# Nodes in 49 blocks of 128 consecutive ones, and edge loads in rows of 64, 3 and 1, in a two-layer graph network kernel

## The chip, the cores and the metric

One core of one Trainium2 chip runs the whole program. The metric is the device time of one execution in microseconds (us); lower is better. The chip's engines that matter here are PE (TensorE, matrix products and transposes), DVE (VectorE), ACT (ScalarE), POOL (GpSimd, which here issues the gathers of table rows) and SP (SyncE, which issues the other transfers in order, in one queue).

## The reference, cut to what matters

There are 6250 nodes with 64 features each and 200,000 edges, sorted by their target `dst`; `src` is random.

```python
h = jnp.maximum(_layernorm(x, axis=-1), 0.0)
# layer 0
t = h @ W0 + b0
agg = segment_sum(edge_weight[:, None] * t[src], dst)      # 6250 x 64
deg = segment_sum(edge_weight, dst)
x = x + relu(agg / (deg[:, None] + 1e-6))
h = jnp.maximum(_layernorm(x, axis=-1), 0.0)
# layer 1
m = gelu(concat(h[src], edge_attr) @ W_msg + b_msg)        # 200000 x 64
agg = segment_sum(m, dst)
x = x + gelu(((1 + eps) * h + agg) @ W_upd + b_upd)
```

## The kernel before, in words

**Edges.** The 200,000 edges are cut into `NG` = 196 groups of 1024, each as `J` = 8 columns of 128 edges. Four groups, one per slot, make a body, and each layer runs 49 bodies. For one group, the rows of the source nodes are fetched into `rows[:, slot, j, :]` in two ways. For six or seven of the eight columns, POOL issues one indirect transfer per column from a table in DRAM (L447; 26 a body in layer 0 and 27 in layer 1). The last column (in some slots the last two) is picked on chip: DVE compares the broadcast source numbers `src_bc` with the node numbers of each partition and writes 0 or 1 into `pick` (L945, function `pick_half`), and PE multiplies these with `parts`, the table split into three bf16 parts, in `NK` = 50 products that add up (L659 `gather`, L666 `extra`). DVE adds the three parts (L973, L979). The comparisons of one pair of groups are made in two halves.

**Sums by target.** Edges are sorted, so a group's targets lie in a window of 72 nodes. ACT makes the one-hot matrix (L523, L527). In layer 0 ACT weights the rows (L553), PE multiplies them with the one-hot (L693), and DVE adds the result to `sums_sb` (L995), which holds features on partitions and nodes along them. In layer 1 PE transposes the edge features (L771), multiplies them with the lower half of `W_msg` (L784, `edge_product`), DVE adds the gathered rows (L1109), and ACT applies gelu (L598). A group whose targets need more windows runs a conditional block on PE and DVE.

**Slots.** POOL fetches into slot `s` for the next body only when `s_used[s]` says that the slot's rows were read (L553 in layer 0, L1109 in layer 1) and `s_idx[s]` that the new indices are there (L461).

**Nodes.** Node `c*625 + p*5 + k` stands on partition p of 125, in chunk c of 10, at place k of 5. So a partition has five consecutive nodes of a chunk, 1280 bytes in DRAM, and a piece of `sums_sb` that belongs to one k is read with a step of five floats (L730, `v[:, k, :]`, and L299, `nodes_of`). Work on nodes goes in five units of two chunks, 640 elements a partition:
- start: SP loads x in five transfers (L310), then src, dst and edge weights, each as 128 + 67 + 1 rows of 4 KB (L314, L315, L317). DVE and ACT do the layer norm; SP stores table 0 (L338). POOL casts src and dst to float (L422 to L426) and then computes `src_last` (L431: the sources of the last two columns minus k, as 16-bit numbers, with ACT's transposed casts `take` at L490 making `src_tab`, `dst_tab` and `w_tab`); SP writes it to DRAM (L341, L343) and loads it back as a broadcast to 125 partitions (L328, L333).
- middle, between the layers: PE multiplies the sums with W0 (L732), DVE divides, adds and normalizes (L1059 to L1063, L851, L852, L858, L863), PE transposes (L751) and multiplies with the upper half of `W_msg` (L758), ACT copies the transposed nodes (L568, L569) and seeds `sums_sb` with them, 50 operations (L578), DVE writes the rows of table 1 (L1072), SP stores them (L391), and POOL starts when all is stored (L437).
- tail: PE multiplies the sums with `W_upd` (L732 again), DVE, ACT and DVE finish (L1136, L611, L1142), SP stores `out` (L406).

Of the kernel before, what the change touches and what calls it, by code (L numbers as in the profile page):

```python
# [5 lines left out]
def two_layer_gnn(  # L6
# [87 lines left out]
    last_src = nc.dram_tensor("last_src", (2, KN, NG, P), i16, kind="Internal").ap()  # L94

    x_view = x.rearrange("(c p k) d -> p c (k d)", p=PN, k=KN)
    out_view = out.rearrange("(c p k) d -> p c (k d)", p=PN, k=KN)
    h0_view = h0_table.rearrange("(c p k) d -> p c (k d)", p=PN, k=KN)
    p1_view = p1_table.rearrange("(c p k) d -> p c (k d)", p=PN, k=KN)


    UC = 2
    UNITS = NC // UC
    UN = UC * KN
    UQ = UN // 2
    UD = UN * D
    BANK = 512
    assert UC * UNITS == NC and UQ == 5
# [3 lines left out]
    with ctx:  # L112
# [3 lines left out]
        def sem(name):  # L116
# [8 lines left out]
        bm_bc = sb("bm_bc", [PN, D])  # L125
        W1b_sb = sb("W1b_sb", [P, P])
        Wu_sb = sb("Wu_sb", [P, D])
        bu_bc = sb("bu_bc", [PN, D])
# [4 lines left out]
        node_f = sb("node_f", [PN, NC])  # L133
        parts = sb("parts", [PN, NK, SPLIT * D], bf16)
        src_bc = sb("src_bc", [PN, 2, KN, PE3 + 16], i16)
        pick_all = sb("pick_all", [P, 2 * NK * PE3], bf16)
        pick = [[pick_all[:, i * NK * PE3:i * NK * PE3 + NK * (PE3 if EXTRA[layer][i] else PE2)].rearrange(
            "p (n e) -> p n e", n=NK) for i in range(2)] for layer in range(2)]
# [5 lines left out]
        def prep(flat, n):  # L144
# [9 lines left out]
        src_tab = sb("src_tab", [P, NG * J], u16)  # L154
        dst_tab = sb("dst_tab", [P, NG * J], i16)
        w_tab = sb("w_tab", [P, NG * J])
        stat = sb("stat", [P, 2, 4])
        stat_i = sb("stat_i", [P, 2, 1], i32)
        once = 10 * G + 2 * P + 2 * KN * P
# [26 lines left out]
        hT = room[:, 0:2 * UQ * PN].rearrange("p (i e) -> p i e", i=2)  # L186
# [7 lines left out]
        psM = [ps[:, 5 + h, 0:J // 2 * D] for h in range(2)]  # L194
        psR = [ps[:, 3:5, :], ps[:, 5:7, :]]
        psU = [ps[:, 1 + 2 * i:3 + 2 * i, :] for i in range(2)]
        psN = [ps[:, 1 + i, :] for i in range(2)]
        psH = ps[:, 5:7, :]
        psP = [ps[:, 0, :], ps[:, 7, :]]
        psS = ps[:, 7, :]  # L200
        psG = [ps[:, 3 + i, 0:SPLIT * D] for i in range(2)]
        psX = ps[:, 2, 0:SPLIT * D]
# [5 lines left out]
        s_wt = sem("edge_weight_loaded")  # L208
        s_const = sem("constants_ready")
# [75 lines left out]
        def unit(t, u):  # L285

            return t[:, u * UC:(u + 1) * UC, :]

        def rows3(t):

            return t.rearrange("p c (k d) -> p (c k) d", d=D)

        def split_to(u):
            return parts[:, u * UN:(u + 1) * UN, :]

        def nodes_of(n):

            c, k = n // KN, n % KN
            return sums_sb[0:D, c * CHUNK:(c + 1) * CHUNK].rearrange("f (p k) -> f k p", k=KN)[:, k, :]  # L299

        @block.sync
        def _(sp):
# [6 lines left out]
            for u in range(UNITS):  # L309
                sp.dma_start(unit(x_sb, u), unit(x_view, u)).then_inc(s_x[u], 16)  # L310
# [41 lines left out]
            sp.dma_start(bm_bc[:, :], b_msg.rearrange("(a n) -> a n", a=1).to_broadcast([PN, D])).then_inc(s_w, 16)  # L352
# [5 lines left out]
            sp.dma_start(bu_bc[:, :], b_upd.rearrange("(a n) -> a n", a=1).to_broadcast([PN, D])).then_inc(s_w, 16)  # L358
# [94 lines left out]
        def _(act):  # L453
# [50 lines left out]
            for s in range(SLOTS):  # L504
                copy_idx(s, s)
# [665 lines left out]
```

## Time and profile before

| | |
|---|---|
| time, median of 3 runs | 3411.88 us (3411.7 to 3414.16) |
| time of the profiled execution | 3412.54 us |
| its span | 3410.7 us |
| busy: PE, DVE, ACT, POOL | 3052.1, 2505.7, 1964.2, 2479.1 us |
| mean granted TensorE clock | 0.967 |
| mean DMA rate | 68 GB/s |

The span is the time from the first to the last instruction of the profiled execution. The busy time of POOL counts the gathers' own time, but not the time between them. "Granted clock" is the share of TensorE's full speed that the chip allowed.

### The profile page before, as it was taken

Reading aid. Unit: us, or ns where it says so; the run is one execution under the profiler, and the core shown is the slowest. Engines: PE = TensorE matmul, PEld = TensorE weight load, DVE = VectorE, ACT = ScalarE, POOL = GpSimd, SP = SyncE. Lnnn points to the kernel's source line nnn. Section 1 sums busy time; section 2 is a strip of 40 time slices with the busy share of each in tenths; the row PEclk is TensorE's granted clock in tenths of the full one; section 3 lists DMA queues with packets and bytes.
Section 4 is the critical chain, followed back from the end, with each engine's and each line's share of the span. In section 5 each row is a group of like instructions: output and inputs, shape, how many; then the busy total and the mean of one; then the engine's idle time right before and its main releaser. Section 6 shows DMA issues by size and latency. Waiting matters only on the chain.

```text
span 3410.7 us, 103092 instructions
## 1 busy us (share of the span) xinstructions
PE 3052.1 (89%) x37471; PEld 2931.5 (86%) x37472; DVE 2505.7 (73%) x3633; ACT 1964.2 (58%) x6688; POOL 2479.1 (73%) x2622
## 2 busy tenths in 40 slices
PE   1999999999999999999879889989999989998998
PEld 1999999999989889989778888888888888888887
DVE  5888777778778778777757767676767677777764
ACT  4666666666665666566565555555555555555553
POOL 4777777777777777777357777777777777777774
PEclk9999999999999999999789999999999999999997
DMA  3333333333333333333123333433333333333331
GB/s 90 74 60 55 57 57 54 54 56 59 54 55 58 56 54 55 57 58 55 36 67 81 80 83 79 84 80 88 76 86 81 79 82 79 81 80 81 79 82 49
DMA packets 336155, 232.77 MB, mean 68 GB/s; under 512 B 141398, under 2 KB 268898, under 8 KB 336126
## 3 DMA queue, kind: packets, MB, share of 16 engines
q0 software_dynamic: 83104, 85.26, 18.1%
q1 hardware_dynamic: 253022, 147.13, 15.6%
q8 instruction: 17, 0.28, 0.0%
q14 instruction: 12, 0.10, 0.0%
HBM read 226.91 MB, written 5.30 MB: 68 GB/s over the span
## 4 chain that ended last, share of the span: by engine, by line
POOL 35%; issue 13%; PE 1%; ACT 1%; DVE 1%; POOLq 0%; DMA 0%; DVEq 0%
POOL rows L447 35%; PE ps L732 1%; ACT sums_sb L578 0%; POOLq L445 0%; DMA p_table<-h_sb 0%; PE ps L758 0%; POOLq L438 0%; DVE pick_all L945 0%; DVE h_sb L852 0%; DVE x_sb L1063 0%; DVE h_sb L1061 0%; DVE ln_m L851 0%; DMA rows<-p_table,idx 0%; ACT sq L468 0%; PE ps L693 0%
## 5 line engine op out<-in xcount | busy, mean ns | idle before, releaser
L945 DVE TENSOR_SCALAR pick_all<-src_bc,node_f 125x1920 bf16<-125x1920 int16 (+1 forms) x1960 | 2067.4, 1121 | 44.9 <-issue 20.4
L659 PE MATMUL ps<-parts,pick_all 125*128 125x192 bf16 x19600 | 1709.8, 248 | 92.2 <-DVE pick_all L945 81.9
L659 PEld LDWEIGHTS ps<-parts,pick_all 125*128 125x128 bf16 x19600 | 1636.1, 99 | 116.0 <-DVE pick_all L945 65.6
L447 POOL DMA_INDIRECT rows<-p_table,idx x1323 | 1249.3, 944 | 424.3 <-issue 424.3
L447 POOL DMA_INDIRECT rows<-h_table,idx x1274 | 1203.2, 944 | 400.5 <-issue 400.2
L523 ACT ACTIVATE onehot<-iota,dw 128x72 f32<-128x72 f32 x3136 | 809.5, 342 | 0.0
L666 PE MATMUL ps<-parts,pick_all 125*128 125x192 bf16 x7350 | 681.4, 252 | 11.6 <-issue 11.4
L666 PEld LDWEIGHTS ps<-parts,pick_all 125*128 125x128 bf16 x7350 | 631.4, 100 | 21.7 <-issue 16.9
L598 ACT ACTIVATE room<-room 128x512 f32<-128x512 f32 x196 | 123.6, 630 | 740.4 <-DVE room L1109 740.4
L1109 DVE TENSOR_TENSOR room<-ps,rows 128x512 f32<-128x512 f32 x196 | 135.6, 692 | 466.3 <-DMA rows<-p_table,idx 437.3
L693 PE MATMUL ps<-onehot,room 128*65 128x72 f32 (+1 forms) x6272 | 381.2, 232 | 92.1 <-ACT room L553 84.6
L693 PEld LDWEIGHTS ps<-onehot,room 128*65 128x65 f32 (+1 forms) x6272 | 333.3, 139 | 136.4 <-ACT room L553 97.8
L553 ACT ACTIVATE room<-rows,dw 128x65 f32<-128x65 f32 x1568 | 397.1, 336 | 59.2 <-DVE rows L973 59.1
L461 ACT CAST idx<-src_tab 128x8 int32 (+1 forms) x392 | 75.8, 194 | 540.4 <-DMA rows<-h_table,idx 539.8
L784 PE MATMUL ps<-W1b_sb,eT 64*128 64x64 f32 x3136 | 217.5, 277 | 89.4 <-issue 88.0
L784 PEld LDWEIGHTS ps<-W1b_sb,eT 64*128 64x128 f32 x3136 | 194.9, 187 | 114.0 <-issue 103.0
L527 ACT ACTIVATE onehot<-onehot 128x576 f32<-128x576 f32 x392 | 268.0, 684 | 12.4
L995 DVE TENSOR_TENSOR sums_sb<-sums_sb,ps 65x72 f32 (+1 forms) x392 | 87.3, 223 | 253.3 <-PE ps L693 253.3
L973 DVE TENSOR_REDUCE rows<-ps 128x64 f32<-128x192 f32 x392 | 136.7, 349 | 56.9 <-PE ps L659 56.6
L771 PE MATMUL ps<-ident,ea 128*128 128x128 f32 x784 | 129.0, 287 | 1.0 <-DVE h_sb L1072 1.0
L593 ACT COPY eT<-ps 128x512 f32<-128x512 f32 x196 | 113.5, 579 | 0.5
L771 PEld LDWEIGHTS ps<-ident,ea 128*128 128x128 f32 x784 | 82.4, 141 | 14.5 <-DVE h_sb L1072 1.3
(90 smaller groups left out, 646.4 us busy)
## 6 DMA issues: line engine op xcount, KB each, us to landing
src_bc<-last_src SPq DMA_DIRECT2D x196, 312.5 KB
ea<-in_edge_attr_dram SPq DMA_DIRECT2D x196, 256.0 KB
src_bc<-last_src SPq DMA_DIRECT2D x147, 156.2 KB
rows<-p_table,idx POOLq DMA_INDIRECT x1323
rows<-h_table,idx POOLq DMA_INDIRECT x1274
x_sb<-in_x_dram SPq DMA_DIRECT2D x5, 312.5 KB
h_table<-h_sb SPq DMA_DIRECT2D x5, 312.5 KB
p_table<-h_sb SPq DMA_DIRECT2D x5, 312.5 KB
```

Of the source, the lines that this page charges most:

```text
L447: nc.gpsimd.indirect_dma_start(out=rows[:, s, j, 0:D], out_offset=None, in_=table[:, :], in_offset=bass.IndirectOffsetOnAxis(ap=idx[:, s, ...
L523: last = nc.scalar.activation(onehot[:, s % 2, j, :], iota[:, :], ACT.Abs, scale=-1.0, bias=dw[:, s, 0, j:j + 1])
L527: nc.scalar.activation(onehot[:, s % 2, :, :], onehot[:, s % 2, :, :], ACT.Relu, scale=-1.0, bias=1.0).then_inc(s_oh[layer], 1)
L553: last = nc.scalar.activation(wrows[:, s % 2, j, :], rows[:, s, j, :], ACT.Copy, scale=dw[:, s, 1, j:j + 1])
L659: last = nc.tensor.matmul(psG[(s + shift) % 2], pick[layer][(s + shift) // 2 % 2][0:PN, n, at:at + P], parts[:, n, :], start=(n == 0), sto ...
L666: last = nc.tensor.matmul(psX, pick[layer][i][0:PN, n, PE2:PE3], parts[:, n, :], start=(n == 0), stop=(n == NK - 1))
L693: last = nc.tensor.matmul(psW[s % 2][at:at + width, :], lhs(j), onehot[:, s % 2, j, :], start=(j < sets), stop=(j >= J - sets))
L771: last = nc.tensor.transpose(psT[:, q * P:(q + 1) * P], ea[:, slot, q * P:(q + 1) * P], ident[:, :])
L784: last = nc.tensor.matmul(psM[h][:, q * D:(q + 1) * D], eT[h * D:(h + 1) * D, q * P:(q + 1) * P], W1b_sb[h * D:(h + 1) * D, h * D:(h + 1) ...
L945: last = nc.vector.tensor_scalar(pick[layer][i][0:PN, c * KN:(c + 1) * KN, :], src_bc[:, i, :, 0:w], node_f[:, c:c + 1], None, ALU.is_equal)
L973: nc.vector.tensor_reduce(rows[:, slot, JG, 0:D], psG[slot % 2].rearrange("p (q d) -> p d q", q=SPLIT), AX.X, ALU.add).then_inc(s_prow[lay ...
L1109: nc.vector.tensor_tensor(pre[:, slot % 2, :].rearrange("p (q h d) -> p q h d", h=2, d=D), ps[:, 5:7, 0:J // 2 * D].rearrange("p h (q d) - ...
```

## The change

Node `n*128 + p` now stands on partition p of 128, in block n of `NB` = 49; the last block has 106 nodes and is padded with zeros. Work on nodes goes in seven units of seven blocks, 448 elements a partition. A block is a contiguous piece of 128 in `sums_sb`, and a row of 256 bytes a partition in DRAM. A pick takes 49 products and seven comparisons of 7 x 384 (or 256) elements, three in the first half and four in the second; the broadcast goes to 128 partitions with seven copies (of src - 128k) in place of five. The remaining 67 rows of an edge load are cut into 64, 3 and 1; the order of the loads is x of units 0 and 1, src, the rest of x, dst, weights. `src_last` is made by 14 ACT operations in place of ten on POOL. POOL's memset of `sums_sb` comes after the src casts. The edge tables are laid out as [column, group], so that the casts write without a step. Seeding takes two ACT operations a unit. `psM` is one bank with four products of 128 columns, not two with eight of 64, and the edge product of the next group is issued right after the first window's products, ahead of the conditional block.

```diff
+    NB = -(-N // P)
+    FULL = N // P
+    TAIL = N - FULL * P
+    KB = 7
+    UNITS = NB // KB
...
+    ROWS2 = (HALF[1] - 1) // 16 * 16
...
-        src_tab = sb("src_tab", [P, NG * J], u16)
+        src_tab = sb("src_tab", [P, J, NG], u16)
...
-        psM = [ps[:, 5 + h, 0:J // 2 * D] for h in range(2)]
+        psM = ps[:, 2, :]
...
+            def blocks(table, lo, hi):
+
+                return table[lo * P:hi * P, :].rearrange("(n p) d -> p n d", p=P)
...
             def load_edges(to, a, loaded):
                 sp.dma_start(to[:, 0, :], a[0:P * G].rearrange("(r e) -> r e", e=G)).then_inc(loaded, 16)
-                sp.dma_start(to[0:HALF[1] - 1, 1, :],
-                             a[P * G:LAST * G].rearrange("(r e) -> r e", e=G)).then_inc(loaded, 16)
+                sp.dma_start(to[0:ROWS2, 1, :],
+                             a[P * G:(P + ROWS2) * G].rearrange("(r e) -> r e", e=G)).then_inc(loaded, 16)
+                sp.dma_start(to[ROWS2:HALF[1] - 1, 1, :],
+                             a[(P + ROWS2) * G:LAST * G].rearrange("(r e) -> r e", e=G)).then_inc(loaded, 16)
                 sp.dma_start(to[HALF[1] - 1:HALF[1], 1, :],
                              a[E - G:E].rearrange("(r e) -> r e", e=G)).then_inc(loaded, 16)
 
+            for u in range(2):
+                sp.dma_start(unit(x_sb, u), blocks(x, u * KB, (u + 1) * KB)).then_inc(s_x[u], 16)
             load_edges(src_raw, src, s_src)
+            for u in range(2, UNITS - 1):
+                sp.dma_start(unit(x_sb, u), blocks(x, u * KB, (u + 1) * KB)).then_inc(s_x[u], 16)
...
+            def store(table, u, done):
+                if u < UNITS - 1:
+                    sp.dma_start(blocks(table, u * KB, (u + 1) * KB), unit(h_sb, u)).then_inc(done, 16)
+                else:
+                    sp.dma_start(blocks(table, u * KB, FULL), h_sb[:, u * KB:FULL, :]).then_inc(done, 16)
+                    sp.dma_start(table[FULL * P:N, :], h_sb[0:TAIL, FULL, :]).then_inc(done, 16)
...
-                sp.dma_start(src_bc[:, i, :, 0:PE2], v.to_broadcast([PN, KN, PE2])).then_inc(s_bc[layer][i], 16)
+                sp.dma_start(src_bc[:, i, :, 0:PE2], v.to_broadcast([P, KB, PE2])).then_inc(s_bc[layer][i], 16)
...
+            nc.gpsimd.memset(sums_sb[:, :], 0.0).then_inc(s_zero, 1)
             pool.wait_ge(s_dst, 64)
...
-            for half in range(2):
-                r = HALF[half]
-                v = src_raw[0:r, half, :].rearrange("r (p j) -> r j p", j=J)[:, JG - 1:J, :]
-                for k in range(KN):
-                    last = nc.gpsimd.tensor_scalar(src_last[0:r, half, :, k, :], v, float(k), None, ALU.subtract)
-            last.then_inc(s_last, 1)
...
             for s in range(SLOTS):
                 copy_idx(s, s)
+            for half in range(2):
+                r = HALF[half]
+                v = src_f[0:r, half, :].rearrange("r (p j) -> r j p", j=J)[:, JG - 1:J, :]
+                for k in range(KB):
+                    last = nc.scalar.activation(src_last[0:r, half, :, k, :], v, ACT.Copy, bias=-float(k * P))
+            last.then_inc(s_last, 1)
...
-                    for n in range(UN):
-                        last = nc.scalar.activation(
-                            nodes_of(v * UN + n), hT[n % 2 * D:(n % 2 + 1) * D, v % 2, n // 2 * PN:(n // 2 + 1) * PN],
-                            ACT.Copy, scale=scale1[n % 2 * D:(n % 2 + 1) * D, 0:1])
-                    last.then_inc(s_seed, 1)
+                    nc.scalar.activation(nodes(v)[:, 0:KB:2, :], hT[0:D, v % 2, :, :], ACT.Copy,
+                                         scale=scale1[0:D, 0:1])
+                    nc.scalar.activation(nodes(v)[:, 1:KB:2, :], hT[D:P, v % 2, 0:QB - 1, :], ACT.Copy,
+                                         scale=scale1[D:P, 0:1]).then_inc(s_seed, 1)
...
-            def sums_product(sums, c, W, width, to):
-                v = sums[:, c * CHUNK:(c + 1) * CHUNK].rearrange("f (p k) -> f k p", k=KN)
-                for k in range(KN):
-                    last = nc.tensor.matmul(to[0:PN, k * width:(k + 1) * width], v[:, k, :], W,
+            def sums_product(u, rows_of, W, width, to):
+                for k in range(KB):
+                    last = nc.tensor.matmul(to[:, k * width:(k + 1) * width], block_nodes(u * KB + k)[0:rows_of, :], W,
                                             start=True, stop=True)
...
                 for q in range(J // 2):
-                    for h in range(2):
-                        last = nc.tensor.matmul(psM[h][:, q * D:(q + 1) * D],
-                                                eT[h * D:(h + 1) * D, q * P:(q + 1) * P],
-                                                W1b_sb[h * D:(h + 1) * D, h * D:(h + 1) * D], start=True, stop=True)
+                    last = nc.tensor.matmul(psM[:, q * P:(q + 1) * P], eT[:, q * P:(q + 1) * P],
+                                            W1b_sb[:, :], start=True, stop=True)
```

## Rows read from the trace of the kernel before

**Rows 1.** The five stages: stretch, its length, busy time by engine, granted clock, DMA share, GB/s.
```profile
0.00:66.70 66.70, 10.34 (x54) 8.78 (x55) 35.26 (x66) 28.24 (x33) 21.24 (x25) 1.00 0.28 90
66.70:1657.80 1591.10, 1477.67 (x17820) 1445.20 (x17820) 1259.45 (x1673) 985.86 (x3917) 1203.19 (x1274) 0.98 0.32 57
1657.80:1724.90 67.10, 43.10 (x195) 39.78 (x195) 42.89 (x74) 40.44 (x87) 5.38 (x3) 0.51 0.12 36
1724.90:3377.00 1652.10, 1497.88 (x19286) 1415.02 (x19286) 1157.97 (x1799) 904.34 (x2641) 1249.25 (x1323) 0.98 0.37 80
3377.00:3410.70 33.70, 23.09 (x116) 22.68 (x116) 10.11 (x25) 5.33 (x11) 0.01 (x1) 0.50 0.16 49
```

**Rows 2.** POOL's gathers by table: duration min/median/max in ns.
```profile
L447 POOL DMA_INDIRECT rows<-p_table,idx x1323: 940/944/1361, 1724.9 to 3376.1; - x189
L447 POOL DMA_INDIRECT rows<-h_table,idx x1274: 940/944/1775, 66.7 to 1656.9; - x182
```

**Rows 3.** Waits over the span: engine, line, for whom; us, times, longest.
```profile
ACT idx L461 <- DMA rows<-h_table,idx: 539.8, 171, 6.4
...
DVE room L1109 <- DMA rows<-p_table,idx: 437.3, 168, 5.9
```

**Rows 4.** Timeline of POOL: start, us, engine, line; the 27th gather.
```profile
100.12 0.94 POOL L447 DMA_INDIRECT rows<-h_table,idx  x1 [0.30 <-issue]
```

**Rows 5.** Timeline of the start, all engines: what was waited for in brackets.
```profile
6.30 0.82 DVE L851 TENSOR_REDUCE ln_m<-x_sb 125x10 f32<-125x640 f32 x1 [4.61 <-DMA x_sb<-in_x_dram]
...
29.40 1.04 POOL L422 CAST pick_all<-pick_all 128x1024 f32<-128x1024 int32 x1 [22.32 <-DMA pick_all<-in_src_dram]
...
33.60 7.09 ACT L490 CAST src_tab<-ps 128x512 uint16<-128x512 f32 x4 [9.60 <-PE ps L622]
...
75.71 10.17 DVE L945 TENSOR_SCALAR pick_all<-src_bc,node_f 125x1920 bf16<-125x1920 int16 x9 [6.67 <-DMA src_bc<-last_src]
...
87.15 6.56 PE L659 MATMUL ps<-parts,pick_all 125*128 125x192 bf16 x50 [25.94 <-DVE pick_all L945]
...
94.20 2.03 ACT L553 ACTIVATE room<-rows,dw 128x65 f32<-128x65 f32 x8 [13.02 <-DVE rows L973]
```

**Rows 6.** Stretches of the start: columns as in rows 1.
```profile
3.00:7.00 4.00, 0.00 (x0) 0.00 (x0) 0.70 (x1) 0.00 (x0) 4.00 (x1) 1.00 0.31 113
20.00:25.00 5.00, 0.00 (x0) 0.00 (x0) 4.19 (x7) 1.15 (x3) 0.00 (x0) 1.00 0.06 26
```

**Rows 7.** Timeline of SP's queue in the start.
```profile
16.25 10.97 SPq L317 DMA_DIRECT2D pick_all<-in_dst_dram  x1
...
39.29 17.10 SPq L338 DMA_DIRECT2D h_table<-h_sb  x5
...
69.22 0.27 SPq L328 DMA_DIRECT2D src_bc<-last_src  x1
```

**Rows 8.** DMA queue from 65.6 to 68 us: packets, MB, share of 16 engines.
```profile
q1 hardware_dynamic: 998, 0.25, 46.5%
```

**Rows 9.** Groups by line and shape: count, busy us, mean ns, idle before.
```profile
L945 DVE TENSOR_SCALAR pick_all<-src_bc,node_f 125x1920 bf16<-125x1920 int16 x1470 | 1673.1, 1204 | 40.3 <-issue 20.4 <-DMA src_bc<-last_src 7.6
...
L945 DVE TENSOR_SCALAR pick_all<-src_bc,node_f 125x1280 bf16<-125x1280 int16 x490 | 394.3, 871 | 4.6
...
L784 PE MATMUL ps<-W1b_sb,eT 64*128 64x64 f32 x3136 | 217.5, 277 | 89.4 <-issue 88.0 <-ACT eT L593 1.4
...
L758 PE MATMUL ps<-W1a_sb,room 128*125 128x128 f32 x50 | 12.5, 434 | 8.7 <-ACT room L569 8.7
...
L1142 DVE TENSOR_TENSOR h_sb<-h_sb,x_sb 125x320 f32<-125x320 f32 x10 | 4.8, 483 | 0.1
```

**Rows 10.** Timeline of middle and tail.
```profile
1665.59 13.20 PE L732 MATMUL ps<-W_sb,sums_sb 65*125 65x65 f32 x60 [1.91 <-DVE tick L1013]
...
1717.32 0.89 DVE L1072 TENSOR_TENSOR h_sb<-ps,bm_bc 125x512 f32<-125x512 f32 x2 [5.18 <-PE ps L758]
...
3382.10 21.86 PE L732 MATMUL ps<-Wu_sb,sums_sb 128*125 128x64 f32 x100 [0.90 <-DVE tick L1013]
```

More of the change, by code:

```diff
@@ L93, in two_layer_gnn @@
     p1_table = nc.dram_tensor("p1_table", (N, D), fp32, kind="Internal").ap()
[L94 to L106, printed above, removed]
+    last_src = nc.dram_tensor("last_src", (2, KB, NG, P), i16, kind="Internal").ap()
+    QB = (KB + 1) // 2
     BANK = 512
-    assert UC * UNITS == NC and UQ == 5
+    assert QB * P == BANK and KB * DA <= BANK
     CONSTS = 7
@@ L124, in two_layer_gnn @@
         W1a_sb = sb("W1a_sb", [P, P])
-        bm_bc = sb("bm_bc", [PN, D])
+        bm_bc = sb("bm_bc", [P, D])
         W1b_sb = sb("W1b_sb", [P, P])
         Wu_sb = sb("Wu_sb", [P, D])
-        bu_bc = sb("bu_bc", [PN, D])
+        bu_bc = sb("bu_bc", [P, D])
         eps_sb = sb("eps_sb", [P, 1])
         scale1 = sb("scale1", [P, 1])
[L133 to L138, printed above, removed]
+        node_f = sb("node_f", [P, UNITS])
+        parts = sb("parts", [P, NB, SPLIT * D], bf16)
+        src_bc = sb("src_bc", [P, 2, KB, PE3 + 16], i16)
+        pick_all = sb("pick_all", [P, 2 * NB * PE3], bf16)
+        pick = [[pick_all[:, i * NB * PE3:i * NB * PE3 + NB * (PE3 if EXTRA[layer][i] else PE2)].rearrange(
+            "p (n e) -> p n e", n=NB) for i in range(2)] for layer in range(2)]
         flat_f = pick_all[:, :].bitcast(fp32)
@@ L403, in _ @@
                     next_bc(1, BODIES - 2, 0)
-            for c in range(0, NC, 2):
-                sp.wait_ge(s_fin, c + 2)
-                sp.dma_start(out_view[:, c:c + 2, :], h_sb[:, c:c + 2, :]).then_inc(s_out, 16)
-            sp.wait_ge(s_out, NC // 2 * 16)
+            for u in range(UNITS):
+                sp.wait_ge(s_fin, u + 1)
+                store(out, u, s_out)
+            sp.wait_ge(s_out, (UNITS + 1) * 16)
         @block.gpsimd
@@ L608, in _ @@
                     copy_dw(1, NG - SLOTS + s + 2, s + 2)
-            for c in range(NC):
-                act.wait_ge(s_fin_b, c + 1)
-                nc.scalar.activation(h_sb[:, c, :], h_sb[:, c, :], ACT.Gelu_apprx_tanh).then_inc(s_fin_g, 1)
+            for u in range(UNITS):
+                act.wait_ge(s_fin_b, u + 1)
+                nc.scalar.activation(unit(h_sb, u), unit(h_sb, u), ACT.Gelu_apprx_tanh).then_inc(s_fin_g, 1)
         @block.tensor
@@ L681, in next_gathers, with windows @@
                     gather(layer, b, s, 1)
-            def windows(layer, b, s, lhs, width, sets):
+            def windows(layer, b, s, lhs, width, sets, between=None):
                 g = b * SLOTS + s
@@ L697, in windows @@
                 product(s_win)
+                if between is not None:
+                    between()
                 count = pe.value_load(row_i[0:1, bass.ds(g, 1), 1], min_val=1, max_val=MAXW)
@@ L942, in pick_half @@
                 w = width(layer, i)
-                for c in range(half * NC // 2, (half + 1) * NC // 2):
-                    last = nc.vector.tensor_scalar(pick[layer][i][0:PN, c * KN:(c + 1) * KN, :], src_bc[:, i, :, 0:w],
+                for c in range(half * UNITS // 2, (half + 1) * UNITS // 2):
+                    last = nc.vector.tensor_scalar(pick[layer][i][:, c * KB:(c + 1) * KB, :], src_bc[:, i, :, 0:w],
                                                    node_f[:, c:c + 1], None, ALU.is_equal)
```

239 lines of the change are left out of this document (112 added, 127 removed).

## The prediction

> **What bounds the kernel now.** I read the stages first [rows 1]: the span falls into a start (66.7 us, until the first gather of layer 0), the gathers of layer 0 (1591.1), a middle (67.1), the gathers of layer 1 (1652.1) and a tail (33.7). PE is busy 93% and 91% of the two long stages, and one would take it for the bound. It isn't. POOL's gathers are issued without a hole: 944 ns each [rows 2] and 0.30 us to the next, so 1591.1/1274 = 1.249 us in layer 0 and 1652.1/1323 = 1.249 us in layer 1. The waits say the same: ACT's copies of indices wait 539.8 us and DVE's message sums 437.3 us for gathered rows to land [rows 3]; PE, DVE and ACT follow POOL. The profiled execution took 3412.54 us for a span of 3410.7; the median of the runs is 3411.88. So 3241 us are a count of gathers that the change leaves alone (26 and 27 a body), and what it can win lies in the other 168 us, and in how early POOL's second round may begin.
>
> That last point matters. The first round (26 gathers) fills four slots; the 27th gather reuses slot 0, once ACT has weighted its rows (L553). It goes out at 100.12 [rows 4], and L553 ended at 94.20 + 2.03 = 96.23 [rows 5]. The consumers had only 3.9 us in hand, so the start is paid twice over: by the table (first gather at 66.7 [rows 1]), and by the chain src_last, its broadcast, picks, first weighted rows.
>
> **The change, part by part.**
>
> *Edge loads.* From 20 to 25 us the core moves 26 GB/s, 6% of 16 DMA engines, that is one engine [rows 6]: a load of 67 rows of 4 KB goes through one alone, 268 KB/26 GB/s = 10.5 us. There are three; SP's next issue sits 10.97 us behind one [rows 7], POOL gets src only at 29.40 [rows 5], and SP starts the table's stores at 39.29 [rows 7], though layer norm is over by 25 (five units of 3.65 from 6.30). Split 64 + 3 + 1, each load takes about 1.5 us. The loads of x run at 113 GB/s with 31% of the engines, five of 16 [rows 6]. The Trainium skill (DMA: Bandwidth & Descriptors, "Why a DMA increments its semaphore by 16 and not by 1") says that a transfer uses the largest number up to 16 that divides its slowest dimension: 5 for 125 rows, 1 for 67, 16 for 128 and 64. By that rule, the trace agrees.
>
> *Blocks of 128.* x, both tables and out now move in pieces of 256 B, not 1280 B. The nearest row is the writing of last_src: 998 packets of 256 B in 2.4 us with 46.5% of 16 engines [rows 8], 17.9 ns each. A unit of 896 costs 896 x 17.9/16 = 1.0 us, where 320 KB at 113 GB/s cost 2.8. Were it 2.0, three places on the path would cost 1 us more each: 3366 at the end. The Trainium skill (DMA: Bandwidth & Descriptors, "Specifications") asks for at least 512 B per transfer for line rate, below which the engine reads, modifies and writes: it speaks against the change and for that second number. 256 B in 17.9 ns is 14 GB/s an engine against 23 with 1280 B, and that loss is in my row already; I keep it.
>
> *Start, in sum.* x unit 0 is there at about 5.1 (before 6.30 [rows 5]). A DVE operation of 640 elements costs 0.82 + 0.03 us (the row at 6.30); 320 cost 0.48 [rows 9]; so 448 cost 0.65. A unit has four, and 0.25 for a reciprocal: 7 x 2.85 = 20.0, with waits 26.1. SP is free by then, and the last store lands by about 31.6: the first gather at 31.6, and the first round is over at 65.
>
> Consumers: ACT finishes layer norm at 25.6, turns src into src_tab in 1.9 us (now written without stride; before 7.09 for four casts [rows 5]), copies idx (28.1), then makes src_last, 14 operations, where POOL had 10. No row shows ACT reading float with a stride: bounds are 0.3 us (dense) and 1.25 us (what a 272-element cast writing with a stride took, from 7.09 split 2.3, 2.3, 1.25, 1.25). I take 0.45, nearer to dense, since the slow casts had 2-byte steps on the writing side, and here the writing is dense: done at 34.4. Two pairs of writes (7/5 of the packets) and landing: 43.3. Broadcast, 896 packets of 512 B on 16 engines instead of 625 on 5: 48.8 (before, issue 69.22 [rows 7], DVE at 75.71 [rows 5]). DVE has its own list: statistics, tables, and now 12 split operations of 0.65 for 8 of 0.85: about 50.3. Picks: 1673.1/1470 = 1.14 us for 1920 elements, 394.3/490 = 0.80 for 1280 [rows 9], so 0.52 ns an element and 1.54 us for 2688; seven are 10.7 us against 11.4. From 61.0 PE's first 49 products take 6.4 (50 took 6.56 [rows 5]), then 0.4 on DVE and 2.1 on ACT: slot 0 free at 70.0, POOL goes at 70.2. Against 100.12: **29.9 us**. The memset moved behind POOL's src casts is hidden: POOL waits for dst there (L425), and without that cover dst's casts come some 5 us later, before DVE wants them at 27. Bounds: 35 if DVE's list and the broadcast both run faster, 21 if strided reads cost as strided writes (14 x 0.65 = 9 us more).
>
> *Loops.* 49 products and 7 picks (3 + 4 to a half) for 50 and 10, four edge products of 128 columns for eight of 64, the edge product ahead of the branch: some 2% off PE and 5% off DVE, all in front of waits for rows [rows 3]: 0. POOL's wait is the cover; if a gather cost under 1.15 us, PE (1477.67/49 = 30.2 us of a body's 32.5 [rows 1]) would take over. Broadcasts grow by 43% in bytes (128 x 7 against 125 x 5), on 16 engines; a later landing has three slots (24 us) of cover.
>
> *Middle.* Before, PE starts sums times W0 at 1665.59, the last table rows come at 1717.32 + 0.89, the first gather at 1724.9 [rows 10, 1]. Sixty products in 13.20 us are 0.22 each, at half clock (0.51 granted, 1.2 GHz [rows 1]), with stationary nodes 5 floats apart. Now they are contiguous. The nearest row with a contiguous 128-wide float stationary and 64 moving columns is L784: 217.5/3136 = 0.069 busy, 0.056 between starts, at clock 0.98 [rows 9, 1]; doubled 0.12. Bounds 0.11 and 0.22. The Trainium skill (SBUF — State Buffer, "Door 1: The DMA port swizzle") gives SBUF lines of 16 bytes and a penalty for each access that crosses into a new one: with a step of 20 bytes each does. By it the penalty goes with the step, and 0.12 follows rather than 0.22, which is rival (b). PE then needs 14 x 0.12 = 1.7 for sums, and for four transposes and eight products of 0.21 (L758: 12.5/50 = 0.25 with its last's end [rows 9]) 2.5, so 4.2 us a unit, the 50 seeding operations on ACT shrink to 14, and DVE sets the pace with seven operations of 0.65 and three short ones (0.7 together): 7 x 5.6 = 39.2 with its wait for ACT's root, 2.0 ahead and 4.8 at the end for transposes, copy and product of the last unit: 46.0 against 52.6. The store saves 1.3 (16 engines, then 106 rows), the last pick of layer 0 is 3 x 1.07 for 5 x 0.80 and its forerunner 4 x 1.54 for 5 x 1.14: 0.4. **8.3 us**, bounds 2 (PE stays at 0.22) and 13.
>
> *Tail.* 100 products in 21.86 us [rows 10] become 98 x 0.12 = 11.9; the last unit's three operations cost 0.4 more, the store 1.3 less: **10.8 us**, bounds 1 and 12.
>
> Sum: 29.9 + 8.3 + 10.8 = 49.0, so 3412.5 - 49.0 = 3363.5; against the median 3362.9. I say 3363.
>
> **Rivals.** (a) The start is held by ACT's strided reads: 9 us less won, 3372. For: strided casts to 2 bytes are three times dense ones; against: those wrote from PSUM. (b) Products on contiguous nodes are no faster, since what costs is the width of the load: no gain in the middle but 2, tail 1: 3380. For: L758, contiguous and 125 wide, takes about as long at this clock [rows 9]; against: it moves 128 columns, not 64. (c) Slower than before: broadcasts on all 16 engines hold up POOL's writing of descriptors. It decides at 49/2597 = 19 ns a gather, 2% of 944. Were a gather to cost 30 ns more, the time would be 3363 + 78 = 3441. Against: 944 in both layers, at 57 and 80 GB/s [rows 1, 2], though the broadcasts keep only five engines busy there. (d) The splitting does not spread the loads: each keeps its 10.5 us, SP's stores start near 39 again, and only middle and tail gain: 3393. Against: loads of 128 rows do spread.
>
> **Chances.** Forecast 0.58, with what beats it; (a) 0.16; (b) 0.14; (c) 0.06, of which 0.04 ends slower; (d) 0.03; no difference, from causes I don't see, 0.03. 0.2% (7 us) is about what a measurement of this kernel can tell. Faster 0.93, same 0.03, slower 0.04. The range runs from 3350 (35 + 13 + 12 and a little) to 3386, which takes in (a) and (b), and leaves out (d), (c) and no difference above it, 0.12, and a little below; of the forecast alone 3353 to 3371.
>
> **What would show it.** Right: first gather near 32, 27th near 70 with a wait for L553; no stretch at 26 GB/s; the gather still 944 ns; PE's products on nodes at 0.12 in middle and tail; the gap between the layers near 58 us, the tail near 23. Wrong: POOL with holes in the loops, a stall on src_bc, a clock under 0.9 in the loops, or src_last ending later than 36.

## The result, and the profile after

The changed kernel takes 3382.18 us (median of 4 runs, 3381.73 to 3383.34), the kernel before beside it 3412.02: ratio 0.9912 [0.9895, 0.9929]. Forecast were 3363, with 3350 to 3386 as the range. So it is faster by 29.8 us where 49 were forecast. The time lies inside the range, but outside the 3353 to 3371 that the prediction gave to its forecast alone, and next to the 3380 of its rival (b). The profiled execution has a span of 3379.9, 30.8 less than before.

Stages of the changed kernel, columns as in [rows 1]:

```profile
0.00:31.10 31.10, 2.85 (x16) 2.69 (x17) 23.04 (x55) 13.81 (x30) 10.91 (x14) 1.00 0.85 181
31.10:1628.10 1597.00, 1445.91 (x17533) 1412.30 (x17534) 1213.57 (x1399) 998.18 (x3943) 1203.45 (x1274) 0.99 0.30 70
1628.10:1696.90 68.80, 49.25 (x236) 42.67 (x233) 47.08 (x90) 25.66 (x61) 5.46 (x3) 0.55 0.17 38
1696.90:3348.30 1651.40, 1498.75 (x17473) 1418.23 (x17473) 1111.61 (x1512) 907.64 (x2643) 1248.49 (x1323) 0.96 0.34 90
3348.30:3379.90 31.60, 22.38 (x114) 21.99 (x114) 9.33 (x19) 4.67 (x8) 0.00 (x0) 0.51 0.26 52
```

Start and first round together gained 29.5 us, with 29.9 forecast (the 27th gather goes out at 70.59 for 100.12). The middle is 68.8 for 67.1 (forecast -8.3, measured +1.7), the tail 31.6 for 33.7 (forecast -10.8, measured -2.1). Its timeline, in the order of time:

```profile
9.53 1.04 POOL L428 CAST pick_all<-pick_all 128x1024 f32<-128x1024 int32 x1 [7.74 <-DMA pick_all<-in_src_dram]
...
27.96 7.80 ACT L510 ACTIVATE pick_all<-pick_all 128x256 int16<-128x256 f32 x14
...
31.10 1.13 POOL L448 DMA_INDIRECT rows<-h_table,idx  x1 [9.35 <-issue]
...
60.93 6.37 PE L664 MATMUL ps<-parts,pick_all 128*128 128x192 bf16 x49 [17.96 <-DVE pick_all L949]
...
70.59 0.94 POOL L448 DMA_INDIRECT rows<-h_table,idx  x1 [5.90 <-ACT room L559]
...
1632.12 1.22 PE L698 MATMUL ps<-onehot,room 128*65 128x72 f32 x16 [1.56 <-ACT room L559]
...
1636.13 3.25 DVE L949 TENSOR_SCALAR pick_all<-src_bc,node_f 128x1792 bf16<-128x1792 int16 x3
...
1639.62 6.64 PE L738 MATMUL ps<-W_sb,sums_sb 65*128 65x65 f32 x30 [6.28 <-DVE tick L1017]
...
3351.14 1.23 PE L698 MATMUL ps<-onehot,room 128*64 128x72 f32 x16 [5.81 <-ACT room L603]
3352.90 21.15 PE L738 MATMUL ps<-Wu_sb,sums_sb 128*128 128x64 f32 x98 [0.53 <-DVE tick L1017]
```

src is on POOL at 9.53 (29.40 in [rows 5]), the first gather goes out at 31.10 and the 27th at 70.59 (100.12 in [rows 4]), which waits for ACT's weighting. The last row says what went wrong in the tail: 98 products on contiguous nodes in 21.15 us are 0.216 each, and 100 in 21.86 were 0.219 [rows 10]. (The trace has two records for each float product, 98 for 49 blocks; "products" with a count are these records here, as in the prediction.)

Some runs below were made on two other chips, where the kernel before took 5814 and 5722 us and variants of the changed one 5336 to 5531. There PE paused between products, and POOL waited for the other engines ("PE-paced chip" below). Of these runs only stretches without such pauses are read, and no whole time of theirs is compared with one from another chip.

### The profile page after: what moved, and what is told of

Same layout as the page of the kernel before. It is cut to its first block, busy times and chain, and to the rows that moved or that the text cites. A ratio compares the mean times of both kernels' runs of the same rounds, so it can differ in the third digit from the quotient of the medians.

```text
span 3379.9 us, 98339 instructions
## 1 busy us (share of the span) xinstructions
PE 3019.1 (89%) x35369; PEld 2897.9 (86%) x35370; DVE 2404.6 (71%) x3073; ACT 1950.0 (58%) x6683; POOL 2468.3 (73%) x2612
## 4 chain that ended last, share of the span: by engine, by line
POOL 36%; issue 13%; PE 2%; DVE 1%; POOLq 0%; ACT 0%; DMA 0%; SPq 0%; DVEq 0%
POOL rows L448 36%; PE ps L738 1%; PE ps L764 0%; POOLq L446 0%; PE ps L755 0%; POOLq L439 0%; DVE pick_all L949 0%; DMA p_table<-h_sb 0%; DMA rows<-p_table,idx 0%; DVE x_sb L1065 0%; DVE h_sb L1063 0%; DVE ln_m L855 0%; DVE h_sb L856 0%; ACT room L575 0%; DVE h_sb L867 0%
## 5 line engine op out<-in xcount | busy, mean ns | idle before, releaser
L949 DVE TENSOR_SCALAR pick_all<-src_bc,node_f 128x2688 bf16<-128x2688 int16 (+1 forms) x1372 | 1960.9, 1489 | 36.2 <-issue 22.3
L664 PE MATMUL ps<-parts,pick_all 128*128 128x192 bf16 x19208 | 1710.4, 251 | 152.9 <-DVE pick_all L949 144.8
L664 PEld LDWEIGHTS ps<-parts,pick_all 128*128 128x128 bf16 x19208 | 1635.4, 100 | 179.2 <-DVE pick_all L949 138.1
L671 PE MATMUL ps<-parts,pick_all 128*128 128x192 bf16 x7203 | 659.7, 250 | 14.2 <-issue 14.1
L671 PEld LDWEIGHTS ps<-parts,pick_all 128*128 128x128 bf16 x7203 | 609.3, 99 | 23.8 <-issue 19.7
L559 ACT ACTIVATE room<-rows,dw 128x65 f32<-128x65 f32 x1568 | 397.1, 336 | 58.0 <-DVE rows L977 57.9
L533 ACT ACTIVATE onehot<-onehot 128x576 f32<-128x576 f32 x392 | 267.9, 684 | 12.4
L787 PE MATMUL ps<-W1b_sb,eT 128*128 128x128 f32 x1568 | 227.0, 288 | 0.0
L787 PEld LDWEIGHTS ps<-W1b_sb,eT 128*128 128x128 f32 x1568 | 189.7, 191 | 15.9
L776 PE MATMUL ps<-ident,ea 128*128 128x128 f32 x784 | 121.3, 277 | 3.0 <-DVE h_sb L1072 0.7
```

The source lines that it names most:

```text
L533: nc.scalar.activation(onehot[:, s % 2, :, :], onehot[:, s % 2, :, :], ACT.Relu, scale=-1.0, bias=1.0).then_inc(s_oh[layer], 1)
L559: last = nc.scalar.activation(wrows[:, s % 2, j, :], rows[:, s, j, :], ACT.Copy, scale=dw[:, s, 1, j:j + 1])
L664: last = nc.tensor.matmul(psG[(s + shift) % 2], pick[layer][(s + shift) // 2 % 2][:, n, at:at + P], parts[:, n, :], start=(n == 0), stop=( ...
L671: last = nc.tensor.matmul(psX, pick[layer][i][:, n, PE2:PE3], parts[:, n, :], start=(n == 0), stop=(n == NB - 1))
L776: last = nc.tensor.transpose(psT[:, q * P:(q + 1) * P], ea[:, slot, q * P:(q + 1) * P], ident[:, :])
L787: last = nc.tensor.matmul(psM[:, q * P:(q + 1) * P], eT[:, q * P:(q + 1) * P], W1b_sb[:, :], start=True, stop=True)
```

## Experiments

**Does the step of a float stationary matter?**

```diff
 def block_nodes(n):
-    return sums_sb[:, n * P:(n + 1) * P]
+    u, k = n // KB, n % KB
+    return sums_sb[:, u * KB * P:(u + 1) * KB * P].rearrange("f (p k) -> f k p", k=KB)[:, k, :]
```

> The changed kernel, but product k of a unit takes as its stationary side every seventh column of the unit's 896 (a step of 28 bytes) in place of 128 contiguous ones, in the middle and in the tail; the sums then belong to permuted nodes. Theory: the stride of a float stationary costs nothing. Then the 98 products of the tail stay at 21.15 us (0.214 each at granted clock 0.50), tail 31.6, middle 68.8, span 3379.9 within 1. Rival: contiguous reading did win something, and something else (the moving side, PSUM) took its place as the limit: then the strided ones are slower, toward 0.3 each, 29 us, span 3388 or more.

The distance between two of DVE's bias additions in the tail is PE's time for one unit. Two neighbours of the run (PE-paced chip), then of the changed kernel, then of the kernel before:

```profile
5468.31 0.62 DVE L1133 TENSOR_TENSOR h_sb<-ps,bu_bc 128x448 f32<-128x448 f32 x1 [2.60 <-PE ps L739]
...
5471.53 0.62 DVE L1133 TENSOR_TENSOR h_sb<-ps,bu_bc 128x448 f32<-128x448 f32 x1 [2.06 <-PE ps L739]
```

```profile
3362.14 0.62 DVE L1132 TENSOR_TENSOR h_sb<-ps,bu_bc 128x448 f32<-128x448 f32 x1 [1.83 <-PE ps L738]
...
3365.13 0.62 DVE L1132 TENSOR_TENSOR h_sb<-ps,bu_bc 128x448 f32<-128x448 f32 x1 [1.83 <-PE ps L738]
```

```profile
3391.04 0.49 DVE L1136 TENSOR_TENSOR h_sb<-ps,bu_bc 125x320 f32<-125x320 f32 x1 [1.28 <-PE ps L732]
...
3393.20 0.49 DVE L1136 TENSOR_TENSOR h_sb<-ps,bu_bc 125x320 f32<-125x320 f32 x1 [1.27 <-PE ps L732]
```

Seven blocks are 14 records (each float product leaves two), five are 10: with a step of 28 bytes 3.22/14 = 0.230 us, contiguous 2.99/14 = 0.214, with a step of 20 bytes and 125 columns 2.16/10 = 0.216. Divided by the columns (128, 128 and 125) that is 1.80, 1.67 and 1.73 ns. Neither theory was quite right: the step of 28 bytes costs 8%, and the one of 20 bytes 4% if the price goes by the column, which no run here tests; not nothing and not half. The Trainium skill (SBUF — State Buffer, "Door 1: The DMA port swizzle") speaks of a penalty for each new 16-byte line and gives no size for it; the prediction made it the step from 0.12 to 0.22, and the rows don't agree, for this kind of read.

**What made the row that I took (L784) so cheap?** (In the tail only, and half of each sum is left out.)

```diff
+    h = k % 2 if u < 4 else 0
+    nc.tensor.matmul(ps[:, 1 + u % 2 + 4 * h, k * D:(k + 1) * D],
+                     block_nodes(u * KB + k)[h * D:(h + 1) * D, :], Wu_sb[h * D:(h + 1) * D, :], ...)
```

> The changed kernel, but the tail's products contract 64 partitions only (one half of the message sums is left out of each): in units 0 to 3 they alternate between the two row halves of the array, each half with its own PSUM bank, in units 4 to 6 all use the same half. Theory: what made the row that the prediction took cheap was that its loads alternate between two halves of the array, which work side by side; then the alternating ones cost 0.11 to 0.13 us each at clock 0.50 and those of one half about 0.21. Rival 1: half the rows is half the price by itself: 0.11 to 0.13 in all seven units. Rival 2: each product at half clock costs 0.21 whatever its rows: 0.21 in all. Where PE falls under 1.3 us a unit, DVE's two operations of 0.65 set the pace, so the distance inside a unit counts; the span falls by 0 to 8 us.

The run (PE-paced chip), the ends of units 2 and 3, which alternate, and of 5 and 6, which use one half:

```profile
5476.20 0.62 DVE L1137 TENSOR_TENSOR h_sb<-ps,bu_bc 128x448 f32<-128x448 f32 x1 [0.55 <-PE ps L822]
...
5477.91 0.62 DVE L1137 TENSOR_TENSOR h_sb<-ps,bu_bc 128x448 f32<-128x448 f32 x1 [0.55 <-PE ps L822]
...
5483.88 0.62 DVE L1137 TENSOR_TENSOR h_sb<-ps,bu_bc 128x448 f32<-128x448 f32 x1 [1.83 <-PE ps L822]
...
5486.87 0.62 DVE L1137 TENSOR_TENSOR h_sb<-ps,bu_bc 128x448 f32<-128x448 f32 x1 [1.83 <-PE ps L822]
```

1.71/14 = 0.122 us each where row halves alternate, 2.99/14 = 0.214 on one half, both at granted clock 0.50: the theory's numbers. L784 in [rows 9] has 64-row halves that alternate (`h` of the old two-bank `psM`), so its 0.056 between starts is two products side by side. The prediction doubled it for half clock, got 0.12, and used it for products that fill all rows.

**The edge loads: the split alone, and all but the split.**

```diff
# in the kernel before (thresholds 48 -> 64)
-  to[0:67, 1] <- 67 rows
+  to[0:64, 1] <- 64 rows;  to[64:67, 1] <- 3 rows
```

> The kernel before, nodes as they were, with the edge loads in rows of 64, 3 and 1 only. Theory: the three loads of 67 rows, each through one DMA engine, held SP's queue and with it both chains of the start, so the split alone brings two thirds or more of the start's 29.5 us: first gather at 43 to 50 in place of 66.7, 27th at 76 to 82 in place of 100.1, span 3387 to 3393. Rival: it is the 128 rows of everything (16 engines for x and for the tables) that brings it: then the split alone leaves the 27th above 90 and the span above 3400.

> The changed kernel with the edge loads in rows of 67 and 1 as before. Theory: 67 rows go through one engine at 26 GB/s, 10.5 us each, three in a row; SP's queue stands behind them, so the table's stores start 8 to 15 us later and the 27th gather goes out at 78 to 88 in place of 70.6; span 3388 to 3397. Rival (each part alone is enough, since x and the loads are also issued in another order now): the 27th within 3 us of 70.6, span at most 3383.

> Edge loads of 67 and 1 rows in the changed kernel and nothing else, again, on a chip where POOL sets the pace. Theory: as the first look showed, the first gather at 55 and the 27th at 95 to 97 in place of 31.1 and 70.6, and all of it reaches the end: span 3404 to 3406, against 3410.7 of the kernel before. Rival: the loops take part of it up: span 3395 or less.

Split alone (PE-paced chip): first gather at 42.24, the 27th at 84.80. But its first picks hit the pauses:

```profile
67.09 6.02 PE L661 MATMUL ps<-parts,pick_all 125*128 125x192 bf16 x43 [19.18 <-issue]
74.14 0.24 PE L661 MATMUL ps<-parts,pick_all 125*128 125x192 bf16 x1 [1.02 <-issue]
75.56 0.32 PE L661 MATMUL ps<-parts,pick_all 125*128 125x192 bf16 x1 [1.18 <-issue]
```

Without them 50 products would end some 6.5 us after 67.09 (6.56 in [rows 5]), and with 2.5 behind them slot 0 would be free at 76 to 77. The 26 gathers ahead are issued by 78.1 in this trace (the last starts at 76.84), so the 27th would go out then: 22 of the 29.5 us, by this estimate. Without the split: 55.48 and 96.49 on a PE-paced chip; where POOL sets the pace 55.0 and 88.39, span 3399.1, median 3399.43, ratio 0.9962 [0.9949, 0.9975]. So 17.2 us of the change's 29.8 hang on the split, less than I expected: the 96.49 that I had carried over held pauses of PE. The first gather is 23.9 us later, but the 27th now follows the 26th without a wait, where it waits 5.90 us in the changed kernel. The two estimates add up to more than the whole, so split and the rest of the change overlap. Why the whole load is so dear shows in the second of these runs, on SP and on DVE:

```profile
3.43 0.91 SPq L307 DMA_DIRECT2D pick_all<-in_src_dram  x1
4.38 13.78 SPq L314 DMA_DIRECT2D x_sb<-in_x_dram  x4
...
27.66 21.79 SPq L324 DMA_DIRECT2D h_table<-h_sb  x6
```

```profile
18.83 0.62 DVE L853 TENSOR_REDUCE ln_m<-x_sb 128x7 f32<-128x448 f32 x1 [11.39 <-DMA x_sb<-in_x_dram]
```

The load itself is issued in under 1 us. What suffers are the loads of x behind it, which are spread over all 16 engines: SP stands 13.78 us in four of them (5.07 in the changed kernel), and DVE waits 11.39 us for the third unit. From 8 to 12 us the core moves 25 to 27 GB/s with 6% to 7% of its engines, the share of one: the other 15 have done their part of x, and x is not complete.

**Layer 1's picks moved behind the middle.**

```diff
-   elif last_body and s == 2:  pick_half(1, 0, 1)
-   elif last_body and s == 3:  dve.wait_ge(s_picked[0], NG); second_pick(1)
    ...
    low(1, u)                       # the last of the middle
+   pick_half(1, 0, 1); second_pick(1)
# SP: "wait s_pick[1] >= 1; load_bc(1, 2, 0)" goes behind the stores of table 1
```

> The changed kernel with layer 1's first pick's second half (4 operations of 1.54 us) and the half behind it (3 of 1.07) made by DVE behind the middle, after the parts of the sums, in place of the last body of layer 0; the broadcast that waits for the pick is issued behind the table's stores. Theory: the middle began late (PE's sums 11.5 us after the last gather's end, 7.8 before) because DVE made these picks ahead of the last windows' sums; without them PE's sums begin 5 to 7 us after the last gather's end, POOL's first gather of layer 1 comes 4 to 6 us sooner, and layer 1's consumers, who had slack of some 19 us, take the 9.4 us: middle 63 to 65, span 3374 to 3376. Rival: the first round of layer 1 lacks that slack, POOL's 28th gather waits and the time is given back: span within 1 of 3380.

> Layer 1's picks behind the middle and nothing else, again, on a chip where POOL sets the pace. Theory: PE's first sums 6 to 8 us behind the start of the last gather of layer 0 in place of 12.4, middle 62 to 64 in place of 68.8, and since the round behind it has slack, all of it is kept: span 3374 to 3376. Rival: the 28th gather of layer 1 waits: span 3378 or more.

The first run (PE-paced chip) had PE's sums at 1.73 us after the last window's products began (7.50 in the changed kernel), but the loops hid the rest. The second: 3376.39 us (ratio 0.9897 [0.9881, 0.9912]), 5.8 less than the changed kernel.

```profile
1632.22 1.22 PE L697 MATMUL ps<-onehot,room 128*65 128x72 f32 x16 [2.02 <-ACT room L558]
1633.94 8.27 PE L737 MATMUL ps<-W_sb,sums_sb 65*128 65x65 f32 x42 [0.51 <-DVE tick L1016]
```

```profile
1628.30:1690.30 62.00, 47.77 (x229) 41.18 (x227) 38.12 (x83) 25.56 (x61) 5.46 (x3) 0.55 0.14 27
1690.30:3342.10 1651.80, 1500.77 (x17473) 1420.89 (x17473) 1121.06 (x1519) 907.48 (x2643) 1248.88 (x1323) 0.96 0.35 90
```

The sums start 6.5 us after the last gather's start, not 12.4, the middle is 6.8 shorter, and in layer 1 POOL never waits longer than its 0.30 us from one gather to the next (1651.8 us for 1651.4). The theory held.

**The clock in tail and middle.** "Fill" is a product of bf16, 128 by 192, on the identity, into a bank that nobody reads.

```diff
+   if last_group: fill(64)          # ahead of the wait for the last messages
    pe.wait_ge(s_msg, ...)
    ...
+   fill(7)
    pe.wait_ge(s_done, 2 * NG + 2)
```

> The changed kernel with 64 products of bf16 (128 by 192, on the identity, into a PSUM bank that nobody reads) ahead of PE's wait for the last messages, and 7 ahead of its last wait, where it stood idle 5.81 and 0.53 us before the tail. Theory A: the tail's products cost 0.213 because the granted clock fell to half while PE stood idle, and float products hold a clock that they find: at clock 1.00 they cost 0.107 to 0.12, tail 20 to 22, span 3369 to 3371. Theory B: float products do not hold the full clock even at 100% busy: it falls again some us into the tail, which saves 2 to 5 us: span 3375 to 3378. Rival: the clock isn't what sets their price: products stay at 0.213 at clock 1.00, span 3380.

> As the run with a warmed tail, and the middle warmed too: 14 such products ahead of PE's wait for the last weighted rows of layer 0, and 66 ahead of its wait for the last sums (idle 1.56 and 6.28 us). Theory A (float products hold a full clock): PE's part of a unit in the middle falls from 7.02 to about 4, DVE sets the pace at 5.4 a unit, middle 58 to 60, span 3359 to 3362. Theory B (they do not): the first units alone gain, middle 64 to 67, span 3371 to 3376. Rival: the middle is DVE's anyway, since it waited only 1.7 us a unit for PE: middle 68, span as with the warmed tail.

Warmed tail (PE-paced chip):

```profile
5392.01 5.44 PE L658 MATMUL ps<-ident 128*128 128x192 bf16 x64
5397.39 0.72 PE L704 MATMUL ps<-onehot,room 128*64 128x72 f32 x16
5398.31 0.75 PE L658 MATMUL ps<-ident 128*128 128x192 bf16 x7 [0.21 <-issue]
5398.90 11.08 PE L744 MATMUL ps<-Wu_sb,sums_sb 128*128 128x64 f32 x98
```

```profile
5400.00:5405.00 5.00, 5.00 (x47) 5.00 (x47) 2.94 (x5) 1.73 (x3) 0.00 (x0) 1.00 0.14 28
5405.00:5410.00 5.00, 4.98 (x45) 4.84 (x44) 3.47 (x6) 1.73 (x4) 0.00 (x0) 1.00 0.77 153
```

The same 98 products in 11.08 us, 0.113 each, at clock 1.00, and 16.9 us from them to the end for 27.0: theory A. With both warmed, the tail is the same again (11.08). In the middle the first 28 products took 3.37 us; the granted clock was 0.98 from 2825 to 2830 and 0.50 from 2830 on, behind idle stretches of 0.83 and 0.27 us with float products on 65 rows between, and each later unit again cost 7.02. That is theory B there: 55.8 us from the first sums to the first gather for 57.3. So fill has to stand inside the units too:

```diff
+   fill(3, 3)                       # ahead of the wait for DVE's sums
    pe.wait_ge(s_x1, u - 1)
    ...
+   fill(30 if v == 0 else 10, 3)
    pe.wait_ge(s_h[1], v + 1)
    ...                              # transposes
+   fill(7, 3)
    pe.wait_ge(s_htc, v + 1)
```

> The changed kernel with bf16 products on the identity ahead of PE's last waits of layer 0 (14 and 74), and inside each unit of the middle, ahead of its waits for layer norm (30 in the first, 10 in the others), for ACT's copy (7) and for DVE's sums (3). Theory: the middle at half clock is PE's (7.02 us a unit, DVE waits 1.7 of them); with no idle stretch the clock stays at 1.00 and DVE's own list sets the pace, 5.3 to 5.5 a unit, so from PE's first sums to the first gather of layer 1 it takes 47 to 49 us in place of 57.3. Rival: float products on 65 rows, or the fill itself, do not keep the clock, or the fill's own time (0.9 us a unit) sits on the path: 54 to 57 us.

3373.35 us, ratio 0.9883 [0.9867, 0.9900], 8.8 less than the changed kernel. Its middle, and one unit of it:

```profile
1642.69 3.26 PE L747 MATMUL ps<-W_sb,sums_sb 65*128 65x65 f32 x28
...
1660.33 1.70 PE L747 MATMUL ps<-W_sb,sums_sb 65*128 65x65 f32 x14
1661.87 0.99 PE L658 MATMUL ps<-ident 128*128 128x192 bf16 x10
1662.70 0.60 PE L766 MATMUL ps<-ident,h_sb 128*128 128x128 f32 x4
1663.13 0.74 PE L658 MATMUL ps<-ident 128*128 128x192 bf16 x7
1664.02 1.30 PE L776 MATMUL ps<-W1a_sb,room 128*128 128x128 f32 x8
1665.25 0.42 PE L658 MATMUL ps<-ident 128*128 128x192 bf16 x3
1665.51 1.70 PE L747 MATMUL ps<-W_sb,sums_sb 65*128 65x65 f32 x14
```

5.18 us a unit for 7.02, DVE's pace, and 46.2 us from first sums to first gather (1688.91) for 57.3. The 74 fill products ahead of the sums ran at half clock at first and took 8.21 us, so that the sums began 14.9 us after the last gather's start, 2.5 later than in the changed kernel. DVE had been ready at 1637.33: this fill held the sums back by over 5 us.

**Everything together.** The first kernel has the moved picks, the fill of tail and units (7 in place of 74 ahead of the sums) and 64 at the start ahead of the first picks; the second has 50 for 14 ahead of the last weighted rows and 96 for 64 at the start.

```diff
+            fill(64, 1)             # second kernel: 96
             gather(0, 0, 0, 0)
     ...
+                    if last_body and s == SLOTS - 1:
+                        fill(14, 6)     # second kernel: 50
                     pe.wait_ge(s_used[s], b + 2)
```

> The changed kernel with all that the runs so far spoke for: picks of layer 1 behind the middle, clock held before and in the middle and before the tail, and 64 more such products at the start ahead of PE's first wait for picks (its first 49 products took 6.4 us at half clock, at full clock 4.2). Where POOL sets the pace as in the traces of before and after: start 2 us shorter, middle 53 to 56 in place of 68.8, tail 21.5 in place of 31.6, span 3352 to 3358. Rival: what the middle gives is taken back at the 28th gather of layer 1, which then waits for slot 0, since its consumers now begin 9 us later: span 3362 to 3368.

> As the kernel with everything, with more of the fill where its trace still showed PE idle and then at half clock: 50 in place of 14 ahead of the last weighted rows of layer 0 (idle 3.5 us there, then 28 products at half clock, 6.1 us), 96 in place of 64 at the start (2.85 us idle behind them, then 5.9 us for the first 49 products). Theory: the 28 products come down to 3.2 us and the 49 to 4.2, so the middle loses 3 us more and the 27th gather goes out at 69: span 3353 to 3355. Rival: DVE sets both places anyway: span as before, 3356 to 3359.

The first: 3356.51 us, ratio 0.9833 [0.9816, 0.9849], middle 56.8, tail 21.6, but the 27th gather still at 70.73. The second: 3355.30, ratio 0.9833 [0.9820, 0.9847].

```profile
61.94 4.21 PE L669 MATMUL ps<-parts,pick_all 128*128 128x192 bf16 x49
...
1632.92 3.34 PE L747 MATMUL ps<-W_sb,sums_sb 65*128 65x65 f32 x28
```

```profile
1627.40:1679.90 52.50, 45.24 (x395) 40.80 (x392) 37.12 (x80) 25.41 (x61) 5.45 (x3) 0.91 0.16 32
1679.90:3332.30 1652.40, 1498.64 (x17487) 1418.63 (x17488) 1120.57 (x1519) 907.84 (x2643) 1249.51 (x1323) 0.96 0.35 90
3332.30:3355.00 22.70, 16.62 (x174) 16.18 (x171) 9.33 (x19) 4.67 (x8) 0.04 (x1) 0.89 0.37 74
```

Both places did what was expected (49 products in 4.21, 28 in 3.34, 27th gather at 69.43), and the profiled span is 3355.0 for 3358.8; by the medians the two kernels can't be told apart. Either is some 26 us under the changed kernel.

## Why the prediction was right and wrong

*What bounds the kernel.* Right (the 3241 us of gathers are 3243.2 by [rows 1], and nothing rests on the slip). The gather stayed at 944 ns. From the 27th gather on, layer 0 took 1557.5 us (1557.7 before), layer 1 1651.4 (1652.1).

*Edge loads and start.* Right, the first gather at 31.1 (31.6 forecast), the 27th at 70.59 (70.2), with the forecast wait for L559. Inside, ACT's strided float reads cost 0.56 each (7.80/14), not 0.45, so `src_last` was ready at 35.8, not 34.4. That did not matter: DVE's own list ended at 50.06 (50.3 forecast), and the broadcast was there. Rival (a) needed 9 us more. Rival (d) is refuted by the rows at 9.53 and by the two runs without the split; what I had not seen is that such a load also holds up the loads over 16 engines behind it.

*Blocks of 128.* Storing and loading in pieces of 256 B cost nothing that shows: the last table rows are written at 1692.76 and the first gather goes out 4.1 us later, where before it took 6.7 (1718.21 to 1724.9). The Trainium skill (DMA: Bandwidth & Descriptors, "Specifications") asks for 512 B or more per transfer for line rate; the prediction took it to speak for its second number, 1 us more at three places, and these rows don't show that.

*Rival (c)*, broadcasts on 16 engines against POOL's descriptors: refuted, 944 ns in both layers at 70 and 90 GB/s.

*Tail, the term of 10.8.* Wrong, by one number: "0.12" for a product on 128 contiguous nodes at half clock. It measured 0.214, and the 98 products took 21.15 us, not 11.9. The row for it was of another shape, 64 rows in alternating halves of the array (the run with half the rows), and contiguous reading is worth 4% to 8%, not half (the run with strided nodes). Rival (b) said this, with 0.14; its row L758, contiguous and at half clock, was the nearer one.

*Middle, the term of 8.3.* Wrong, by two numbers. A unit on PE, from the changed kernel:

```profile
1657.82 1.06 PE L755 MATMUL ps<-ident,h_sb 128*128 128x128 f32 x4
...
1659.60 2.27 PE L764 MATMUL ps<-W1a_sb,room 128*128 128x128 f32 x8 [0.72 <-ACT room L575]
...
1661.79 3.25 PE L738 MATMUL ps<-W_sb,sums_sb 65*128 65x65 f32 x14
```

The unit is 7.02 us where 4.2 were forecast: 3.05 for the sums (1.7 forecast), and 3.97 for the four transposes, the wait for ACT's copy and the eight products (2.5 forecast, without a wait). Either error alone would have left DVE's 5.6 a unit as the pace, or nearly: 3.0 + 2.5 = 5.5, and 1.7 + 4.0 = 5.7. Together they kept PE the pace, and DVE waited for it; from the first sums to the last table rows it took 53.1 us, as before (52.6), where 46.0 were forecast.

So the time is in the range because the range was drawn wide enough for rival (b), and not because the working of middle and tail held.

*Middle, the picks.* A third error: I counted the last pick 0.4 cheaper. DVE makes a half of four (6.16 us) and one of three (3.25) around the last windows, and PE's first sums came 11.5 us after the last gather's end where they had come 7.8 after. Moving them away gave 6.8, so nothing covers them in the changed kernel. The middle's sum is then 3.73 more ahead of the sums, 0.52 more in the units, 2.55 less for the store (1.3 forecast): the 1.7 measured. Why did the part ahead grow, though the kernel before made its picks there too? The trace after shows ACT waiting 6.00 us for a slot's gathered rows (until 1617.01) while 85% of the DMA engines were busy with the wider broadcasts (1610 to 1615), then PE idle for 3.72 us and its clock at 0.50 (1620 to 1625); before, PE waited 1.80 us there and kept its clock. The run with fill in the units, which has none ahead of this stretch, tells the two apart: ACT waits as long (6.12 us, until 1617.66) and PE is idle as long (3.80), but the granted clock is 1.00 from 1620 to 1625. DVE's last sum then ends 9.5 us after the last gather's start, for 12.3 in the changed kernel and 8.6 before. So some 2.8 of the 3.7 us go with the clock, by this comparison of two single executions; the rest, and why the clock fell in one and not in the other, stay open.

*The sum.* 29.5 of 29.9, -1.7 of 8.3, 2.1 of 10.8, and loops and edges of stages 0.9: 30.8 of 49.0.

## What to carry to other kernels

Before a row serves as a price, compare the shape behind it: rows of the array used, what its neighbours in the queue are, and the granted clock; a distance between starts may be two instructions side by side. Where a stage runs at clock 0.50, ask what the engine did before it fell: in the tail the price of products was a matter of 5.8 us of idling ahead of them, worth 10 us, and in the middle of idle stretches within the units, worth 11 from the first sums to the first gather. The layout gave 2 and none. In a forecast of a pipeline, count the handovers too: a wait of 0.72 us a unit was left out here. A load whose rows go through one DMA engine is paid for by the loads behind it.

## What the runs showed of the hardware

Float products on 128 rows did not bring the clock back and did not lose it in the tail: at 0.50 they ran 21.15 us back to back and it stayed 0.50; found at 1.00, it stayed 1.00 for 11.08 us. In the middle, on 65 rows and with short idle stretches between, they lost it; whether by the rows or by the idling no run tells. The Trainium skill (TensorE: Matmul & The Clock Gate, "What's actually happening") says that the slow clock is the default and activity releases it; for bf16 products the trace agrees (in the changed kernel, 0.50, 0.78 and 1.00 in 1700 to 1705, 1705 to 1710 and 1710 to 1720, while PE ran the first picks of layer 1), for these float products it doesn't.

Float products on 64 rows at half clock: 0.214 us if all use one half of the array, 0.122 if they alternate between halves.

On two chips PE paused within its loops, mostly one to three products and then 0.2 to 2.2 us of nothing, with a granted clock of 0.71 to 0.88 over stretches of 100 us; gathers kept their 944 ns. There POOL waited for the other engines, and variants of the changed kernel took 0.938 to 0.947 of the kernel before (the split alone 0.9964 [0.9943, 0.9985]). What the pauses come from no run here shows.
